# Layer 0's opening rearranged: stacks by groups, low halves on VectorE, batch 1's projections in the loop, its rotary sums on GpSimd

## The reference

```python
mod = (silu(L0_c) @ L0_wmod).reshape(4, 6, 1, 256)
sa, ca, ga, sb, cb, gb = (mod[:, j] for j in range(6))
ga = (2 * (ga >= 0) - 1) * maximum(abs(ga), 0.25)
h = layernorm(x) * (1 + ca) + sa
q, k, v = (h @ w.T + b for (w, b) in ((wq, bq), (wk, bk), (wv, bv)))   # 16 heads of 16
q, k = rope(q, k)           # even channels: even * cos - odd * sin; odd channels stay
attn = softmax(q @ k.T / sqrt(16))
x = x + ga * ((attn @ v) @ wo.T + bo)
```

## Time and profile before

| | |
|---|---|
| median of 3 runs | 1400.22 us (1394.95 to 1400.45) |
| profiled execution, own time | 1403.09 us |
| its span, first to last instruction | 1401.8 us |
| TensorE busy | 1268.2 us (90%), 6431 instructions |
| VectorE / ScalarE / GpSimd busy | 868.7 / 779.1 / 411.3 us |
| mean granted TensorE clock | 0.960 |
| layer 0's loop, first to last scores | 50.1 to 286 us |
| barrier behind layer 0's attention | about 321 us |

### The profile page before, as it was taken

One profiled execution on the slowest core, in us unless ns is written; L12 is line 12 of the kernel. 1 busy time (PEld: TensorE's weight loads), 2 busy tenths in 40 slices (PEclk: granted clock), 3 DMA queues, 4 the chain that ended last, 5 costly groups with the idle time before them and its releaser, 6 DMA issues.

```text
span 1401.8 us, 22438 instructions
## 1 busy us (share of the span) xinstructions
PE 1268.2 (90%) x6431; PEld 896.4 (64%) x6431; DVE 868.7 (62%) x2629; ACT 779.1 (56%) x1911; POOL 411.3 (29%) x516
## 2 busy tenths in 40 slices
PE   6679998888799998999999999999999979999994
PEld 5334443335457776777777777777877755678773
DVE  5568888845642364775676566666666755433555
ACT  3257776663423445776667666665666643256552
POOL 5313423100445544200010125001600151455553
PEclk9589999998899998999999999999999998999997
DMA  6632717315114542145000001000100019555764
GB/s 204 156 63 48 153 37 147 88 37 230 53 53 134 161 142 95 62 152 155 20 1 16 1 16 47 1 16 1 58 4 16 1 57 384 176 144 157 208 198 134
DMA packets 77399, 134.06 MB, mean 96 GB/s; under 512 B 11977, under 2 KB 50897, under 8 KB 75609
## 3 DMA queue, kind: packets, MB, share of 16 engines
q1 hardware_dynamic: 62368, 92.65, 21.5%
q0 software_dynamic: 13664, 38.08, 9.7%
q10 hardware_dynamic: 1248, 1.90, 0.4%
HBM read 77.03 MB, written 60.00 MB: 98 GB/s over the span
## 4 chain that ended last, share of the span: by engine, by line
PE 67%; DVE 14%; issue 7%; ACT 5%; DMA 3%; POOL 3%; another core or an unknown queue 0%; DVEq 0%; SPq 0%; ACTq 0%; POOLq 0%
PE psum L127 8%; PE psum L129 8%; PE psum L2028 8%; PE psum L128 8%; PE psum L2689 6%; PE psum L2735 4%; PE psum L1999 4%; PE psum L2562 4%; PE psum L855 3%; PE psum L884 3%; PE psum L2596 2%; POOL results L2758 2%; DVE psum L1963 2%; PE psum L779 2%; DVE a_nmax L791 1%
## 5 line engine op out<-in xcount | busy, mean ns | idle before, releaser
L1974 ACT ACTIVATE a_spare<-psum,a_nmax 128x128 f32<-128x128 f32 (+3 forms) x256 | 134.8, 527 | 92.7 <-DVE a_nmax L1963 81.7
L791 DVE TENSOR_REDUCE a_nmax<-psum 128x2 f32<-128x1024 f32 x128 | 155.1, 1217 | 48.3 <-PE psum L779 47.1
L870 ACT ACTIVATE a_et<-psum 128x512 f32<-128x512 f32 x256 | 138.9, 595 | 66.0 <-PE psum L855 62.3
L2028 PE MATMUL psum<-a_et,a_v 128*128 128x512 f32 (+3 forms) x512 | 170.1, 434 | 1.6 <-DVE a_ctx L2045 1.3
L2758 POOL DMA_INDIRECT results<-r_fin,r_to x134 | 134.3, 1002 | 126.2 <-issue 59.0
L1963 DVE CUSTOM_DVE_ANT_0 psum<-psum,a_spare 128x128 f32<-128x128 f32 (+3 forms) x256 | 127.0, 496 | 63.5 <-PE psum L129 54.4
L2689 PE MATMUL psum<-m_w,m_xT 128*128 x536 | 150.4, 403 | 0.0
L2008 ACT ACTIVATE a_et<-psum 128x128 f32<-128x128 f32 (+3 forms) x256 | 111.3, 435 | 44.9 <-PE psum L1999 39.8
L127 PE MATMUL psum<-a_kT,a_q 128*128 128x128 f32 (+3 forms) x256 | 118.6, 463 | 0.7 <-ACT a_spare L1974 0.7
L855 PE MATMUL psum<-a_stk 52*128 52x512 f32 x256 | 104.6, 475 | 14.0 <-ACT a_et L870 10.3
L1999 PE MATMUL psum<-ident,a_spare 128*128 128x128 f32 x640 | 113.0, 274 | 2.5 <-DVE a_spare L1987 2.3
(11 more groups left out here) (332 smaller groups left out, 2925.9 us busy)
## 6 DMA issues: line engine op xcount, KB each, us to landing
r_xs<-slots SPq DMA_DIRECT2D x134, 129.0 KB
slots<-empty SPq DMA_DIRECT2D x12, 1290.0 KB, 6.7
m_w<-in_experts SPq DMA_DIRECT2D x16, 768.0 KB
stacks<-a_qk SPq DMA_DIRECT2D x32, 256.0 KB, 3.7
a_stk<-stacks POOLq DMA_DIRECT2D x32, 256.0 KB, 4.7
r_shared_hid<-results SPq DMA_DIRECT2D x12, 512.0 KB
m_w<-in_experts SPq DMA_DIRECT2D x4, 1216.0 KB
a_stk<-stacks POOLq DMA_DIRECT2D x32, 128.0 KB, 5.2
```

The lines of the kernel that those rows point to most:

```text
L791: dve.tensor_reduce(nmax[:, G % 2, qt, 2 * p:2 * p + 2], psum[:, n:n + 2, :], AX.X, ALU.max, negate=True).then_inc(s_max.sem, 1)
L870: act.activation(et[:, n % NET, 2 * p + hh, :], psum[:, 4 + hh, :], ACT.Exp).then_inc(s_e.sem, 1)
L1974: act.activation(e[:, u % NE, 0:W], psum[:, n, 0:W], ACT.Exp, bias=nmax[:, u % NE, :], scale=-1.0, accum_out=rsum[:, u % NE, :]).then_inc( ...
L2028: mm = pe.matmul(psum[:, n, kt * P:S], v[:, b % 2, kt, h // HPG1 * HD1:(h // HPG1 + 1) * HD1], queries(i, kt), start=(kt == 0), stop=(kt = ...
```

## The change

Only `attention0` and helpers that it alone calls are changed; lines below the loop's end are as before.

- **Loads.** SyncE issues the bias ahead of the rotary table, then x of batch 1, the rest of the modulation weights, bo and bv (with a semaphore of their own), `w0_o`, and x of batches 2 and 3.
- **Activation tables.** A one-element Sqrt is run after silu, and a one-element Exp just ahead of the loop.
- **TensorE filler.** `tensor_warm` issues 5 matmuls of zeros (256 columns, float32) ahead of the first modulation, 3 behind the transposes, 4 ahead of the loop.
- **Batch 0's halves.** VectorE makes the low halves of the three weight stages and of h by halves, and those of q and k; ScalarE and VectorE take one half of h's scale and shift each. The first projection waits for h's halves one by one.
- **Stacks by groups.** Head half 0 of q and k is written first. Of it, the part of group 0 (two of four pairs) is loaded first: queries by GpSimd (4 DMAs), keys by SyncE (2) and GpSimd (2). Then come head half 1's writes and the rest of the loads.
- **Batch 1.** Its statistics, normalised rows, transposes and low halves stand ahead of the loop (four buffers of xn for two); its four projections take steps 0 to 7, half a projection a step, its values steps 8 to 11. The even products stay on VectorE (steps 4 and 8), the odd product and the sum are GpSimd's (steps 9 and 13), the halves are at 11 and 15, the writes at 12 and 16, the loads of its first stacks at 15 and 19. Keys get a buffer of their own.
- **Modulation.** Its second part stays ahead of the loop on TensorE; VectorE copies it out at step 14 with the bias sum; the gates are made at step 39.

The core of the diff:

```diff
+        act.wait_ge(*k.eps_ready)
+        act.activation(k.lnw[:, 1, 0:1], k.eps[:, :], ACT.Sqrt).then_inc(k.sem("act_warm").sem, 1)
...
         for j in range(n_w):
             scalar_stage(j)
-            gpsimd_stage(j)
...
+        def tensor_warm(n, bank):
+
+            pe.wait_ge(*k.empty_ready)
+            if g.free[bank]:
+                pe.wait_ge(*g.free[bank])
+            for _ in range(n):
+                mm = pe.matmul(psum[:, bank, 0:D], k.empty[:, 0:P], k.empty[:, 0:D], start=True, stop=True)
...
+        def vector_stage(j):
+            src, hi, lo, c = staged[j]
+            s = k.sem("dve_half_lo")
+            dve.wait_ge(*stage_in[j, "hi"])
+            dve.tensor_tensor(lo[:, c * S:(c + 1) * S], stage(j), hi[:, c * S:(c + 1) * S],
+                              ALU.subtract).then_inc(s.sem, 1)
...
+        def gpsimd_rope_sum(b, i):
+            s, a = s_turned, turned(b, i)
+            pool.wait_ge(*o_ready[b, i])
+            pool.tensor_tensor(a[:, 2, :], a[:, 1, :], rope[:, 2, :], ALU.mult).then_inc(s.sem, 1)
+            pool.wait_ge(*s.up())
+            pool.wait_ge(s_ropeE.sem, s_ropeE.n)
+            pool.tensor_tensor(a[:, 2, :], a[:, 0, :], a[:, 2, :], ALU.add).then_inc(s.sem, 1)
+            e_ready[b, i] = s.up()
...
+        tensor_warm(5, WARM_BANK)
+        first = g.next()
+        modulated = tensor_modulation(k, 0, 0, outs[0], wmod[0], first, None)
+        pe.wait_ge(*k.ident_ready)
+        for n in range(TT):
+            norm.vector_xn(0, n, n)
+            norm.tensor_turn(0, n, g)
+        vector_stage(0)
+        g.free[first] = vector_modulation(k, 0, outs[0], first, modulated)
+        tensor_warm(3, WARM_BANK)
+        scalar_first_h(1)
+        vector_first_h(0)
+        vector_stage(1)
+        norm.scalar_hi(0)
+        for i in range(KT):
+            vector_first_lo(i)
+        vector_stage(2)
...
+        for i in range(2):
+            scalar_rope(0, i)
+            vector_rope_odd(0, i)
+            vector_rope_even(0, i)
+            vector_rope_sum(0, i)
+            scalar_halves(0, i)
+            vector_halves(0, i)
+            sync_to(0, i, (0,))
+        early, rest = slice(0, 2), slice(2, HALF0)
+        queries_in = load_stack(pool, s_first, 0, 0, early)
+        keys_in = load_stack(sp, s_keys, 0, 1, early, (0,))
+        more_in = load_stack(pool, s_first, 0, 1, early, (1,))
+        for i in range(2):
+            sync_to(0, i, (1,))
...
+        norm.vector_stats(range(TT, 2 * TT), TT)
+        norm.scalar_sd()
+        norm.vector_rstd()
+        for n in range(TT):
+            norm.vector_xn(1, n, TT + n)
+        norm.vector_stats(range(2 * TT, NT), 2 * TT)
+        modulated = tensor_modulation(k, 0, 1, outs[1], wmod[1], MOD_BANK, g.free[MOD_BANK])
...
+        for half in range(2):
+            tensor_rows(1, half, ROWS_BANKS[half])
+        biased = tensor_bias(MOD_BANK)
+        tensor_warm(4, WARM_BANK)
+        for half in range(2):
+            scalar_rows(1, half)
+            scalar_rows_hi(1, half)
+            vector_rows_lo(1, half)
...
+        FIRST_V, FIRST_SUM, FIRST_HALVES, FIRST_MOD, GATES_AT = (8, 10), (9, 13), (11, 15), 14, 39
...
+            if 0 <= s < 8:
+                j, kt = divmod(s, KT)
+                tensor_qk(1, j // 2, 1 - j % 2, (kt,), ROWS_BANKS[j // 2] if j % 2 else None)
+            for pair in range(2):
+                if 0 <= s - FIRST_V[pair] < 2:
+                    tensor_v(1, pair, (s - FIRST_V[pair],), ROWS_BANKS[pair])
...
-        for s in range(XN_AT[0] - SOONER, PER_BATCH * B + 31):
+        for s in range(PER_BATCH * B + 31):
```

More of the change, by code:

```diff
@@ L548, in turned @@
         def turned(b, i):
+            if b == 1 and i:
+                return second
             return later if b else first_two[:, i]
@@ L701, in gpsimd_halves, with vector_halves, sync_to @@
                 lo_ready[b, i] = s_qklo.up()
-            if b:
-                work_free[0] = lo_ready[b, i]
-        def sync_to(b, i):
+            work_free[work(b, i)] = lo_ready[b, i]
+        def vector_halves(b, i):
+            s = k.sem("dve_half_lo")
+            for odd in (1, 0):
+                dve.wait_ge(*hi_ready[b, i, odd])
+                dve.tensor_tensor(qk[:, i, 2 + odd, :], turned(b, i)[:, 2 - odd, :], qk[:, i, odd, :],
+                                  ALU.subtract).then_inc(s.sem, 1)
+                lo_ready[b, i] = s.up()
+        def sync_to(b, i, halves=range(2)):
             sp.wait_ge(*lo_ready[b, i])
-            for half in range(2):
+            for half in halves:
                 for hh in range(2):
@@ new lines, in attention0 @@
+        tensor_warm(3, WARM_BANK)
[7 more added lines that the diff above has]
+        for i in range(2):
+            for odd in (1, 0):
+                tensor_qk(0, i, odd)
+        for half in range(2):
+            tensor_v(0, half)
+        for i in range(2):
[6 more added lines that the diff above has]
+            sync_to(0, i, (0,))
@@ new lines, in attention0 @@
+        stk_in[0, 0] = keys_in, more_in
+        for i in range(2):
+            gpsimd_stack(1, i)
+        norm.vector_stats(range(TT, 2 * TT), TT)
[5 more added lines that the diff above has]
+        modulated = tensor_modulation(k, 0, 1, outs[1], wmod[1], MOD_BANK, g.free[MOD_BANK])
+        lo_of_split = {0: norm.split_ready[0]}
+        for half in range(2):
+            tensor_rows(1, half, ROWS_BANKS[half])
@@ L1135, in ahead @@
         def ahead(s, at):
[L1137 to L1138 removed]
+            for b in range(2, B):
+                d = s - PER_BATCH * (b - 1)
                 if d in at:
@@ L1241, in scalar @@
                 norm.scalar_sd()
+            if s in (2, 6):
+                scalar_rope(1, s // 4)
+            if s in FIRST_HALVES:
+                scalar_halves(1, FIRST_HALVES.index(s))
+            for pair in range(2):
+                if s == FIRST_V[pair] + 2:
+                    scalar_v(1, pair)
             for b, half in ahead(s, ROWS_AT):
```

276 lines of the change are left out of this document (159 added, 117 removed).

## The result

The changed kernel's median is 1393.0 us in 22 runs (1382.0 to 1408.4) against 1399.4 us of the kernel before in as many (1393.4 to 1406.2). The ratio is 0.9944, interval 0.9925 to 0.9962: faster by some 0.6%, or 8 us, where 22 had been forecast. The ratio leaves out the three slowest runs of the changed kernel (1404.1, 1404.6 and 1408.4, over 1.5% above its fastest); the median of its other 19 is 1391.5. The profiled execution took 1390.24 us.

The account below looks back on a forecast made before the run. It took latency in the opening's 50 us chain of waits as the bound, then TensorE's loop. Gains 14.9 + 4.4 + 4.0 - 1.0 = 22.3 us took the profiled 1403.1 to 1380.8, the median to 1378; range 1370 to 1391.

Parts of the forecast that it names:

- Part 1: Opening up to TensorE's first projection: at 14.8 us instead of 18.7, a gain of 3.9.
- Part 2: Opening up to the low halves of the keys: 24.9 us instead of 32.7, with 24 matmuls in 7.
- Part 3: Stacks and step 0: first scores at 35.2 us instead of 50.1, 14.9 won; far end 40.
- Part 4: Loop steps 0 to 13: 19.4 us instead of 23.8, a gain of 4.4; bounds 17.4 and 26.4.
- Part 5: Loop steps 13 to 25: 21.6 us, a gain of 4.0, with 2.8 for GpSimd; bounds 18.8 and 25.6.
- Part 6: Gates made on VectorE at step 39: 1.0 us lost, bounds 0 and 1.8.
- Sum: Whole kernel: 14.9 + 4.4 + 4.0 - 1.0 = 22.3 us won, median 1378.
- One of my own signs of being wrong: First scores after 41 us, loop clock staying near 0.7, or step 25's gain gone by the barrier.
- A: Rival: stacks arrive near 40 us and TensorE meets the moved projections at half clock; 11 won, 1389; chance 0.17.
- B: Rival: work merely moved, steps 0 to 11 at half clock, step 0 at 40; about 6 won, 1394; chance 0.06.
- C: Rival: slower, GpSimd's queue in a row with two stack-load landings, 28.7 us lost, 1404; chance 0.04.
- D: Rival: opening filler of zeros does not bring full clock, 3.3 us more before the loop, 1381; chance 0.03.

Follow-up runs that it names:

- e4: Changed kernel without its twelve filler matmuls of zeros in the opening: median 1393.9 us, ratio 0.9939 to the kernel before.
- e2: Changed kernel with 16 filler matmuls in a row at step 20: median 1389.6 us, ratio 0.9926 to the kernel before.
- e17: Changed kernel with only batch 1's first stack loads two steps later, at steps 17 and 21: median 1390.3 us, ratio 0.9925 to the kernel before.
- e9: The changed kernel run again without an edit: median 1390.9 us, ratio 0.9939 to the kernel before.
- e10: Changed kernel with batch 1's second values at steps 19, 20 and GpSimd's sums at 4, 9, halves at 8, 12: 1383.2 us, ratio 0.9886.
- e14: Repeat of the changed kernel with second values at 19, 20 and GpSimd's sums at 4, 9, halves at 8, 12: 1382.7 us, ratio 0.9885.
- e5: Changed kernel with GpSimd's batch 1 sums at steps 4, 9 and halves at 8, 12: median 1392.0 us, ratio 0.9903 to the kernel before.
- e11: Changed kernel with later second values, sooner GpSimd sums and halves, and two filler matmuls at each of steps 13 to 15: 1390.8 us, ratio 0.9919.
- e13: Changed kernel with later second values, sooner GpSimd work, bias matmuls ahead of batch 1's transposes and six fillers behind: 1383.1 us, ratio 0.9884.
- e1: Changed kernel with two filler matmuls at each of steps 13, 14 and 15: median 1390.6 us, ratio 0.9929 to the kernel before.
- e6: Changed kernel with 17 steps of filler matmuls between steps 13 and 30: median 1402.9 us, ratio 0.9956 to the kernel before.
- e12: Changed kernel with later second values, sooner GpSimd work, filler at steps 13 to 15 and more filler in the opening: 1389.1 us, ratio 0.9925.
- e18: Repeat of the changed kernel with GpSimd's sums at steps 4, 9 and halves at 8, 12: median 1384.6 us, ratio 0.9893.
- e3: Changed kernel with the second half of batch 1's values back at steps 19 and 20: median 1387.6 us, ratio 0.9898 to the kernel before.
- e15: Changed kernel with only a longer dense stretch ahead of step 0 (bias matmuls before transposes, six fillers instead of four): 1389.1 us, ratio 0.9917.
- e7: Changed kernel with GpSimd's sums and halves sooner and filler at steps 13 to 30: median 1395.6 us, ratio 0.9921 to the kernel before.
- e8: The kernel before with filler of the same kind at steps 13 to 30: median 1410.2 us, ratio 1.0011 to the kernel before.

## Why the prediction was wrong

**Part 1** was right in its order and 1.8 us too late: 13.04 for 14.8. The five small steps took the 1.0 us; four normalised tiles took 1.38 us (0.41 each, as forecast, but each begins before the last has ended: 0.35 from start to start). The modulation took 2.05 us instead of 3.58; that was the filler's doing, since in e4 it took 3.57 and the first projection came at 14.38. The eight transposes took 1.95 us where I had 2.5, with the filler and, in e4, without: the 0.31 that I had read from the earlier trace rows held waits for VectorE's tiles.

**Part 2**: 22.4 for 24.9, the start passed on and 24 matmuls in 5.6 us instead of 7.

**Part 3**: first scores at 34.5 for 35.2, but by two errors against each other, so the number was luck. The halves were 2.5 us sooner, and the first load of the keys was issued only at 28.7, 6.3 us behind the low half, where I had 3.4 to 4.8. I had taken 2.8 to 4.2 and 4.8 to 6.7 us for the ranges of writes and loads, which are the shortest and the median. The write in the chain took 7.9 us, longer than any there, and it is the queries', issued at 19.1, not the keys': GpSimd issues its loads in order behind it. The last load landed in 4.3 us, sooner than any of the earlier trace rows. One of my three chains, the DMAs', set step 0, by another path than I had drawn.

**Part 4**: 19.1 for 19.4, with 3.5 us at half clock. This too is one profile: the same program took up to 28.6 us there (e2, e17), beyond my far bound of 26.4.

**Part 5 is the step that failed.** "At the later pace it would be 12 x 1.57 = 18.8", and 2.8 us for GpSimd: 21.6. Measured 29.1, and 8.2 us more lost from step 25 to 40, which I had taken as kept. I had named GpSimd's queue and priced it well for itself (1.8 to 3.2 us of TensorE's time). What I missed is the pace: 1.57 us a step is the pace at a granted clock of 1.00, and steps 13 to 25 ran at 0.53, steps 25 to 40 at 0.66. The clock was lost at the light steps just before the wait, or in it (e9), and the loop ran at half clock for 51 us. I treated the clock of the kernel before as a fault of its own opening, to be healed by starting earlier, and counted its going as a gain. Much of the low time of the kernel before lay where TensorE waited anyway, from 34.6 to 65.3 us, with TensorE busy for only 17.7 of 30.7 us:

```profile
34.60:65.30 30.70, 17.71 (x52) 10.94 (x53) 17.32 (x48) 6.14 (x11) 9.67 (x17) 0.50 0.59 139
```

But that half clock was cheaper in it is not shown within the loop: its steps 0 to 40 took 75.7 us with 28 low, where the line of the change's relatives gives 76.2, and its runs have the same slope. What differs is how long the clock was low: 55 us instead of 28 within steps 0 to 40, and (55 - 28) x 0.31 = 8.4 us. Of the 15.5 us won by step 0 that would leave 7.1; 8.4 were left. The 1.3 between is not taken apart. e10 and e14 agree with it: in the change with two things moved, 12 and 17 us low, 19.7 and 18.3 us are left at step 40, near the 22.3 forecast. That the half clock took these us is so read from the traces and the slope; what made it fall and stay is open.

**Part 6**: 1.0 was about right. At full clock, steps 25 to 40 took 27.7 us in e2, e5, e10, e11, e13, e14 and e17 with the gates in them, against 26.4 before: 1.3.

**Sum.** The terms up to step 13 add up to 20.2 us won for 19.3 forecast. In steps 13 to 40 the forecast fell short by 7.6 + 8.2 - 1.0 = 14.8, and 0.9 more had been won up to there: 8.4 left at step 40 for 22.3. One of my own signs of being wrong came: the loop's clock stayed near 0.7 (0.67 from step 0 to 40).

**The rivals.** A had the right size (1389) and named a meeting at half clock, but at the wrong place: the stacks were not late. B's steps 0 to 13 at half clock (nearly) throughout are not in the result's profile but in those of e2, e4, e5, e11 and e17 (27.7 to 29.5 us); its late step 0 is in none. C had the right queue and a price of 28.7 us in a row; the waiting itself was 1.8 to 3.2. D can be denied: the filler did bring the full clock (0.23 us a matmul from the first on; in e4 0.43 for ten of them), and no effect on the time can be told. The range ended at 1391, 2 us short of the median. It should have held a low stretch behind step 13 as long as the earlier trace rows showed one for half of the steps there (0.73 of 25.6 us is 14 us low), and twice as long.

The Trainium skill's "TensorE: Matmul & The Clock Gate" (HAM oscillation — how this bites in real kernels) describes a kernel that falls to half rate at each wait for a DMA and starts its next work there. The falls inside waits of 3.1 to 4.3 us for GpSimd (e1, e6, e9) and for SyncE's row (e10, e12, e13, e14, e18) agree with it. The falls of the first profile, of e3 and of e15 are another case: they came 5.5 to 9.3 us ahead of the wait for GpSimd, and TensorE had stood still for no more than 0.9 us at a time in the 15 us before them.

**Open.** Which of GpSimd's orders and the values' place gives how much: together 0.9885, alone 0.989 to 0.990, with wide intervals and runs in two clusters. What lets the clock fall without a long wait, and what brings it back at 107 us in one execution and at 71 in another, no run tells. The returns gather at few steps (16; 18 to 20; 22; 28 in e1, e3, e4, e7 and e15; 32 to 34), and ahead of that at 107.2 TensorE had been busy without a gap for 4 us, but it had been so for 5.5 us from 56.0 on as well. The profiled pair differs by another 4.8 us behind step 124 (1116.0 against 1120.8 us), which the profiles of the change's relatives spread over as well (1113.8 to 1127.8, part of it by chip); I did not follow it.

## What to carry to other kernels

When a change takes waits out ahead of a loop that TensorE bounds, do not count the full clock of a later stretch as won: price each us at half clock from the traces, here 0.31 us, and give the low stretches a range of their own. Then look for the places where TensorE stands still for 2 to 4 us inside such a loop, and at the queue (GpSimd's loads, SyncE's writes) in which its small release stands behind large ones. GpSimd's part done sooner and the second values later, together, won as much here as the whole change; which of the two it was is not shown. Judge by many runs: two profiles of one and the same kernel had this stretch at different places.

## What the runs showed of the hardware

- A loop in which TensorE is busy 33.5 of 36 us stayed at a granted clock of 0.50 for 51 us (56 to 107 us), and other executions of like kernels for 75 us (e4) or 10 us (e14).
- The time of a run follows its mean granted clock at 9 us for 0.01, with a correlation of -0.93, in the kernel before and in the change alike; most of the spread from 1382 to 1408 us goes with it. In e8 and e12, six runs each, it does not show (-0.27 and -0.15).
- The clock fell inside a wait of TensorE of 3.1 to 4.3 us in eight profiles (e1, e6, e9, e10, e12, e13, e14, e18), and in three (the first of the change, e3, e15) with no wait over 0.9 us in the 15 us before.
- With GpSimd idle meanwhile, VectorE normalised a tile in 0.41 us in the change as in the earlier trace rows; the slowed ones, beside GpSimd's subtractions, had taken 1.30.
